# A fused conditional-FFN kernel: the conv's condition term as ScalarE's bias instead of column sums of W, W split by chunk, another unit order in the first iteration

## The chip, the cores and the metric

The kernel runs on one core of a Trainium2 chip. The metric is the device time of one execution in microseconds (us). Each core has TensorE (PE, the matmul engine; PEld is its weight load), VectorE (DVE), ScalarE (ACT), GpSimd (POOL) and SyncE (SP), each with its own queue of instructions, and 16 DMA engines. Engines work in parallel and meet only at semaphores. On-chip memory is SBUF; matmuls write to the banks of PSUM.

## What is computed

Two layers, each adding a feed-forward of a conditional mixing to its input x (128 images, 64 channels, 1024 positions):

```python
x = x + _L0_ffn_ref(_L0_cond_ref(x, cond_128, ...), A, B, bias)   # per-image 64x64 mix + bias, then (.) @ (A @ B.T).T + bias
x = x + _L1_ffn_ref(_L1_cond_ref(x, cond_128, ...), W_up, gate_w, expert_bias, lora_A, lora_B)
# _L1_cond_ref: out = conv1d(x, weight, 9 taps, 4 groups); ctx = c @ c_weight.T
#               out = out + ctx[:, :, None] + bias[None, :, None]
# _L1_ffn_ref:  out @ W_up.T  +  LoRA delta (rank 8) of the one expert that the gate picks (argmax of 4 logits)
```

The condition term ctx + bias is one number for each image and output channel of the conv. It is the same at all 1024 positions.

## The kernel before

The 128 images go in 32 super-steps s of four images; a super-step has two tiles t = 2s and 2s + 1 of 128 rows each. All fp32 products are made of two parts, a rounded high part (fp32r, made by a ScalarE copy) and the low rest (a VectorE subtraction), in three matmuls: high x high, high x low, low x high.

Layer 0 of a super-step: `unit_u` (x times B), `unit_tu` (transposes), `unit_v` (the per-image mix), `unit_o(s, i)` (times A, four banks F0 to F3, into which ScalarE has put the bias). VectorE's `addx` adds the result to x1. SyncE's queue then copies parts of x1 into `Xr` (`rx`, 16 DMAs per super-step), VectorE takes differences (`xd`), ScalarE and VectorE split them (`xs`).

Layer 1, the conv: for each of four groups g, `unit_p(s, g)` makes a product shared by even and odd positions (L778, 3 matmuls, bank F4; in super-step 0 also O1), ScalarE's `pc(s, g)` copies it, doubled, into bank F[g], and `unit_c(s, g)` (L790, 6 matmuls) accumulates on top of it. VectorE transposes the result (`ty`), and `ys` splits it into `yh` and `yl`. Then `step_c(t, c, k)` (L805) multiplies a tile with W (three chunks of 292, 512 and 256 columns, 8 row blocks k each, 3 matmuls per step). The first 36 columns are the gate's and LoRA's; VectorE's `zc` picks the expert, `unit_zt` transposes, ScalarE copies (`zst`), `unit_dl` (L824) adds the LoRA product, and VectorE's `f` adds x1 and writes the output tile.

The condition term is not added to the conv's output in this version. Its effect behind W is: condition value times the sum of W's column block. `wsum` (L840, L841) makes those column sums by 48 matmuls with a matrix of ones in the start-up; they become rows 96 to 98 of `Ls`, the condition values (`cbn`, `cb3`) become columns 96 to 98 of `zs`, so that the LoRA product with 99 rows adds them. For the 36 gate columns `zc` adds `gsB` times `cbn`.

The order on each engine is written out by hand. The loop over `it` runs 32 iterations; iteration `it` has 48 steps n (24 for tile 2·it, 24 for tile 2·it + 1), and between the steps stand the units of later super-steps at fixed n: u(it+2) at 3, tu at 7, v at 9, o(it+2) at 13 to 16, products p(it+1) at 16, 18, 22, 26, convs c(it+1) at 18, 21, 26, 30. Where both stand at one n, the conv comes first. In the start-up, W comes in 8 DMAs, one for each row block with all 1060 columns (`w(k)`: high part by ScalarE, low by VectorE); `wsum`, all of super-step 0's products and convs and o(1) stand ahead of the first step. The lines with the waits that matter here:

```python
def unit_p(s, g):                     # before; s > 0
    if g == 0: pe.wait_ge(v_v, ...)
    elif s > 0: pe.wait_ge(a_pc, 4 * s + g)      # bank F4 is free once ScalarE has copied product g - 1
def unit_c(s, g):
    pe.wait_ge(a_pc, 4 * s + g + 1)
```

## Time and profile before

| | |
|---|---|
| time, median of 3 runs | 1201.2 us (1200.6 to 1202.0) |
| profiled execution | 1200.4 us, span 1198.7 us |
| TensorE busy | 1161.1 us, 97% |
| VectorE busy | 756.0 us, 63% |
| ScalarE busy | 436.8 us, 36% |
| DMA, mean | 127 GB/s; queue 1 takes 46% of the 16 engines |
| granted TensorE clock, mean | 0.988 |

The page gives the busy time of each engine, the span in 40 slices, the DMA queues, the chain of work that ended last, and the costliest groups of instructions by line. TensorE's share of the chain is 94%, most of it in L805. Busy time by stretch tells the start-up from the loop; the chain and the timelines show single instructions and what each waited for. A matmul's duration in a timeline includes its pipeline; what it costs in a row of matmuls is the distance between two starts.

### The profile page before, as it was taken

Reading aid. Unit: us, or ns where it says so; the run is one execution under the profiler, and the core shown is the slowest. Engines: PE = TensorE matmul, PEld = TensorE weight load, DVE = VectorE, ACT = ScalarE, POOL = GpSimd, SP = SyncE. Lnnn points to the kernel's source line nnn. Section 1 sums busy time; section 2 is a strip of 40 time slices with the busy share of each in tenths; the row PEclk is TensorE's granted clock in tenths of the full one; section 3 lists DMA queues with packets and bytes.
Section 4 is the critical chain, followed back from the end, with each engine's and each line's share of the span. In section 5 each row is a group of like instructions: output and inputs, shape, how many; then the busy total and the mean of one; then the engine's idle time right before and its main releaser. Section 6 shows DMA issues by size and latency. Waiting matters only on the chain.

```text
span 1198.7 us, 18813 instructions
## 1 busy us (share of the span) xinstructions
PE 1161.1 (97%) x7460; PEld 1058.4 (88%) x7460; DVE 756.0 (63%) x1511; ACT 436.8 (36%) x669; POOL 8.9 (1%) x22
## 2 busy tenths in 40 slices
PE   6569999999999999999999999999999999999998
PEld 5467999999999999999999999999999999999998
DVE  4847666666766666766566676666667666666652
ACT  5544333334433333433333343333244333334320
POOL 2000000000000000000000000000000000000000
PEclk9789999999999999999999999999999999999999
DMA  9724544544454454445445445544543554544211
GB/s 324 225 63 107 144 113 136 140 117 102 134 147 113 133 142 113 106 135 138 121 133 142 108 107 140 126 130 136 139 101 115 143 114 138 140 124 106 64 52 53
DMA packets 113723, 151.75 MB, mean 127 GB/s; under 512 B 21356, under 2 KB 91500, under 8 KB 109388
## 3 DMA queue, kind: packets, MB, share of 16 engines
q1 hardware_dynamic: 113028, 148.36, 46.4%
q10 hardware_dynamic: 608, 2.20, 0.5%
q8 instruction: 59, 0.97, 0.3%
q14 instruction: 28, 0.23, 0.1%
HBM read 80.87 MB, written 35.68 MB: 97 GB/s over the span
## 4 chain that ended last, share of the span: by engine, by line
PE 94%; DVE 3%; ACT 1%; SPq 1%; DMA 1%; issue 0%; DVEq 0%; ACTq 0%
PE O L805 62%; PE F L790 8%; PE F L758 7%; PE F L778 4%; PE O L824 3%; PE F L730 2%; PE F L729 2%; PE F L728 2%; DVE Wl L588 1%; SPq L222 1%; PE O L816 1%; PE F L745 1%; PE F L746 1%; DMA Xr<-x 0%; DVE wks L609 0%
## 5 line engine op out<-in xcount | busy, mean ns | idle before, releaser
L805 PE MATMUL O<-Wh,yh 128*128 128x292 f32 (+2 forms) x1536 | 510.4, 332 | 0.0
L805 PE MATMUL O<-Wh,yl 128*128 128x292 f32 (+2 forms) x1536 | 498.5, 325 | 0.0
L805 PE MATMUL O<-Wl,yh 128*128 128x292 f32 (+2 forms) x1536 | 498.2, 324 | 0.0
L805 PEld LDWEIGHTS O<-Wh,yh 128*128 128x128 f32 x1536 | 290.0, 189 | 22.9
L805 PEld LDWEIGHTS O<-Wh,yl 128*128 128x128 f32 x1536 | 289.7, 189 | 23.2
L805 PEld LDWEIGHTS O<-Wl,yh 128*128 128x128 f32 x1536 | 290.5, 189 | 17.1
L579 DVE TENSOR_TENSOR osb<-O,x 128x256 f32<-128x256 f32 (+1 forms) x192 | 97.6, 508 | 107.2 <-PE O L824 107.2
L300 ACT ACTIVATE F<-F 128x512 f32<-128x512 f32 x126 | 73.3, 582 | 241.8 <-PE F L778 241.7
L536 DVE STREAM_TRANSPOSE yr<-F 128x512 f32<-128x512 f32 x128 | 91.1, 712 | 58.8 <-PE F L790 58.8
L300 ACT ACTIVATE u<-F 128x256 f32<-128x256 f32 x64 | 24.5, 383 | 267.1 <-PE F L730 223.5
L510 DVE TENSOR_TENSOR x<-F,x 128x512 f32<-128x512 f32 x128 | 87.9, 689 | 36.1 <-PE F L758 36.1
L519 DVE TENSOR_TENSOR Xd<-Xr 128x512 f32<-128x512 f32 x64 | 43.9, 685 | 67.9 <-DMA Xr<-x 67.9
L728 PE MATMUL F<-xTh,Bh 128*128 128x256 f32 x256 | 73.5, 287 | 8.7 <-DVE xTl L478 8.7
L300 ACT ACTIVATE yh<-yr 128x1024 fp32r<-128x1024 f32 x64 | 67.6, 1056 | 32.1 <-DVE yr L536 32.1
L544 DVE TENSOR_TENSOR yl<-yr,yh 128x1024 fp32r<-128x1024 f32 x64 | 77.9, 1218 | 1.8 <-ACT yh L300 1.8
L527 DVE TENSOR_TENSOR Xl<-Xd,Xh 128x1024 fp32r<-128x1024 f32 x64 | 78.0, 1218 | 0.0
L790 PE MATMUL F<-Xh,Th 128*128 128x256 f32 x256 | 75.3, 294 | 1.7 <-ACT F L300 1.7
L478 DVE TENSOR_TENSOR xTl<-xTr,xTh 128x1024 fp32r<-128x1024 f32 x64 | 76.5, 1199 | 0.0
L729 PE MATMUL F<-xTl,Bh 128*128 128x256 f32 x256 | 73.1, 285 | 0.0
L730 PE MATMUL F<-xTh,Bl 128*128 128x256 f32 x256 | 73.0, 285 | 0.0
L790 PE MATMUL F<-Xh,Tl 128*128 128x256 f32 x256 | 71.4, 279 | 0.0
L790 PE MATMUL F<-Xl,Th 128*128 128x256 f32 x256 | 71.3, 278 | 0.0
(139 smaller groups left out, 1520.5 us busy)
## 6 DMA issues: line engine op xcount, KB each, us to landing
x<-in_xP_dram SPq DMA_DIRECT2D x64, 516.0 KB, 4.8
Xr<-x SPq DMA_DIRECT2D x512, 64.5 KB, 2.5
xTr<-in_xT_dram SPq DMA_DIRECT2D x32, 1024.0 KB, 6.5
out_dram<-osb SPq DMA_DIRECT2D x64, 512.0 KB, 2.9
Wr<-in_Wd_dram SPq DMA_DIRECT2D x8, 530.0 KB, 14.1
agb<-agb_scratch SPq DMA_DIRECT2D x31, 128.0 KB, 3.3
agg_scratch<-stage ACTq DMA_DIRECT2D x1, 2048.0 KB, 8.3
agg<-agg_scratch SPq DMA_DIRECT2D x60, 32.0 KB, 2.5
```

Source lines behind the costliest of these rows:

```text
L300: return act.activation(dst, src, ACT.Copy)
L510: dve.tensor_tensor(dst, F[i][:, :].rearrange("p (c a) -> p c a", c=4), dst, ALU.add).then_inc(v_x1, 1)
L527: dve.tensor_tensor(Xl[:, q, 0:2], Xd[:, q, 0:2], Xh[:, q, 0:2].bitcast(fp32), ALU.subtract).then_inc(v_xs, 1)
L536: dve.transpose(yr[:, t % YR].rearrange("p (k r) (g b n) -> p g b k r n", r=2, g=2, b=4)[:, g % 2], F[g][:, :].rearrange("p (b i) -> p b i ...
L544: dve.tensor_tensor(yl[:, t % YR], yr[:, t % YR], yh[:, t % YR].bitcast(fp32), ALU.subtract).then_inc(v_yl, 1)
L579: dve.tensor_tensor(osb[:, lo:hi, :], O[c][:, OFF[c]:CH[c][1]].rearrange("p (c a) -> p c a", c=hi - lo), xs_, ALU.add).then_inc(v_f, 1)
L728: pe.matmul(F[4][:, 0:256], Bh[:, c, :], xTh[:, c, :], start=c == 0, stop=False)
L729: pe.matmul(F[4][:, 0:256], Bh[:, c, :], xTl[:, c, :], start=False, stop=False)
L730: last = pe.matmul(F[4][:, 0:256], Bl[:, c, :], xTh[:, c, :], start=False, stop=c == 7)
L758: last = pe.matmul(F[i][:, :], w[:, q].rearrange("p g b n -> p (g b n)"), m[:, 4 * h:4 * h + 4, :].rearrange("p c a -> p (c a)"), start=Fa ...
L790: last = pe.matmul(dst[:, e], w[:, g, e, :], m[:, g // 2, e, b0:b0 + 4, :], start=False, stop=n_ == 2, skip_group_check=True)
L805: last = pe.matmul(O[c][:, 0:w_], w[:, t % YR, k, :], m[:, k, c0:c0 + w_], start=k == 0 and n_ == 0, stop=k == 7 and n_ == 2)
```

## The change

- The condition term is added at its place: ScalarE's `pc` adds it as a bias column (`cbX`, one value for each partition, group and image) when it copies the shared product. The bias belongs to one image, so the copy of a bank becomes four ACTIVATEs of 128 columns (Identity with a bias column).
- `cbX` is made by four matmuls of 128 columns (`ccX` times condT) behind unit_v(0) and four VectorE additions. `wsum`, `gsB`, `cbn`, `cb3`, three rows of `Ls` and three columns of `zs` go, with their copies.
- W comes in six pieces by chunk and half of the row blocks (`WP`), so that the first chunk can be used before the last has come. `step_c` of tile 0 waits for the piece that it uses.
- Start-up and first iteration get another order on all engines: products 2 and 3, convs 2 and 3 of super-step 0 and o(1) move behind the first steps; the units of super-steps 1 and 2 stand later in iteration 0. `Lr` lies over `osb`; `onesr` and `Xr2` lie elsewhere over `yl`.
- In iterations 1 to 31 the convs stand at 19, 21, 26, 30 (before 18, 21, 26, 30), the products at 16, 18, 22, 26 as before.

```diff
+WP = [(0, 0, 4), (0, 4, 8), (1, 0, 4), (1, 4, 8), (2, 0, 4), (2, 4, 8)]
...
-            return O[1] if s == 0 and g % 2 == 1 else F[4]
+            return O[1 + g % 2] if s == 0 else F[4]
...
-            for k in range(8):
-                sp.dma_start(Wr[:, k, :], Wd[:, k, :]).then_inc(d_w[k], 16)
+            for j, (c, k0, k1) in enumerate(WP):
+                c0, w_ = CH[c]
+                sp.dma_start(Wr[:, k0:k1, c0:c0 + w_], Wd[:, k0:k1, c0:c0 + w_]).then_inc(d_w[j], 16)
...
-                copy(F[g][:, :].rearrange("p (b e i) -> p b e i", b=4, e=2),
-                     pbank(s, g)[:, 0:256].rearrange("p (b i) -> p b i", b=4).unsqueeze(2).broadcast_to([128, 4, 2, 64])).then_inc(a_pc, 1)
+                if s == 0 and g == 0:
+                    act.wait_ge(v_cb, 4)
+                for b in range(4):
+                    last = act.activation(F[g][:, 128 * b:128 * b + 128].rearrange("p (e i) -> p e i", e=2),
+                                          pbank(s, g)[:, 64 * b:64 * b + 64].unsqueeze(1).broadcast_to([128, 2, 64]),
+                                          ACT.Identity, bias=cbX[:, g, 4 * s + b:4 * s + b + 1])
+                last.then_inc(a_pc, 1)
...
+            w(0)
             ut(0)
...
             tuu(0)
-            w(0)
+
+            act.wait_ge(v_wk, 4)
+            w(1)
             vhi(0)
...
             copy(Th[:, :, :, :], Tr[:, :, :, :]).then_inc(a_t, 1)
-            for k in range(1, 4):
-                w(k)
-
-            act.wait_ge(v_wk, 4)
-            w(4)
-            w(5)
             txh(1)
-            w(6)
-            w(7)
-            act.wait_ge(d_l, 16)
-            copy(Ls[0:96, :], Lr[:, :]).then_inc(a_l, 1)
-
-            act.wait_ge(p_cb, 2)
+            w(2)
+            w(3)
+
+            act.wait_ge(p_cb, 1)
...
-                dve.scalar_tensor_tensor(out=zl[:, :], in0=gsB[:, :], scalar=cbn[:, t // 2, t % 2:t % 2 + 1], in1=O[0][:, 0:36],
-                                         op0=ALU.mult, op1=ALU.add).then_inc(v_z, 1)
-                if t > 0:
-                    dve.wait_ge(p_zt, t)
-                dve.tensor_copy(zs[:, 96:99].bitcast(f32r), cb3[:, t, :])
+                dve.tensor_copy(zl[:, :], O[0][:, 0:36]).then_inc(v_z, 1)
...
-                if t == 0 and k == 0:
-                    pe.wait_ge(v_ws, c + 2)
+                if t == 0 and k % 4 == 0:
+                    pe.wait_ge(v_w, 2 * c + k // 4 + 1)
+                if t == 0 and c == 0 and k == 0:
+                    pe.wait_ge(v_cb, 4)
...
-            wsum(0)
-            wsum(1)
-            wsum(2)
-            pe.wait_ge(v_ws, 3)
             unit_p(0, 0)
             unit_p(0, 1)
             unit_c(0, 0)
-            unit_p(0, 2)
             unit_c(0, 1)
-            unit_p(0, 3)
-            unit_c(0, 2)
-            unit_c(0, 3)
-            for i in range(4):
-                unit_o(1, i)
             for it in range(NS):
                 for n in range(48):
                     t = 2 * it + n // 24
                     step_c(t, n % 24 // 8, n % 8)
-                    if n == 3:
+                    if it == 0 and n in (1, 2):
+                        unit_p(0, n + 1)
+                    if it == 0 and n in (3, 4):
+                        unit_c(0, n - 1)
+                    if it == 0 and n in (5, 6, 7, 8):
+                        unit_o(1, n - 5)
+                    if n == (9 if it == 0 else 3):
                         unit_u(it + 2)
...
-                    if n in (18, 21, 26, 30):
-                        unit_c(it + 1, {18: 0, 21: 1, 26: 2, 30: 3}[n])
-                    if n in (16, 18, 22, 26):
-                        unit_p(it + 1, {16: 0, 18: 1, 22: 2, 26: 3}[n])
+                    no = 18 if it == 0 else 13
+                    if no <= n < no + 4:
+                        unit_o(it + 2, n - no)
+                    pp, cc = ((24, 27, 41, 44), (26, 29, 43, 46)) if it == 0 else ((16, 18, 22, 26), (19, 21, 26, 30))
+                    if n in cc:
+                        unit_c(it + 1, cc.index(n))
+                    if n in pp:
+                        unit_p(it + 1, pp.index(n))
```

How the built orders differ at three places. The first is TensorE in an iteration of the loop, from product 0 (first row) on; of three matmuls in a row the first stands. F4 and F0 are PSUM banks, O2 the third chunk's bank. Before:

```order
L778 MATMUL F4<-Xh_85,Th_58 128x256 [waits v_v,v_xs]
...
L805 MATMUL O2<-Wh_49,yh_86 128x256
...
L790 MATMUL F0<-Xh_85,Th_58 128x4x64 [waits a_pc]
...
L778 MATMUL F4<-Xh_85,Th_58 128x256 [waits a_pc]
...
L805 MATMUL O2<-Wh_49,yh_86 128x256
```

After:

```order
L820 MATMUL F4<-Xh_83,Th_58 128x256 [waits v_v,v_xs]
...
L849 MATMUL O2<-Wh_49,yh_84 128x256
...
L820 MATMUL F4<-Xh_83,Th_58 128x256 [waits a_pc]
...
L849 MATMUL O2<-Wh_49,yh_84 128x256
...
L832 MATMUL F0<-Xh_83,Th_58 128x4x64 [waits a_pc]
```

Product 1 now stands ahead of conv 0 with a step between them. Next, ScalarE in an iteration of the loop, the copies of the shared products of one super-step. Before:

```order
L300 ACTIVATE F0<-F4 128x512 [waits v_x1,p_p]
L300 ACTIVATE F1<-F4 128x512 [waits v_x1,p_p]
L300 ACTIVATE F2<-F4 128x512 [waits v_x1,p_p]
L300 ACTIVATE yh_86<-yr_88 128x1024 [waits v_ty]
L300 ACTIVATE F3<-F4 128x512 [waits v_x1,p_p]
```

After:

```order
L369 ACTIVATE F1<-F4,cbX_65 128x128 [waits v_x1,p_p]
L369 ACTIVATE F1<-F4,cbX_65 128x128 x3
L369 ACTIVATE F2<-F4,cbX_65 128x128 [waits v_x1,p_p]
L369 ACTIVATE F2<-F4,cbX_65 128x128 x3
L300 ACTIVATE yh_84<-yr_86 128x1024 [waits v_ty]
L369 ACTIVATE F3<-F4,cbX_65 128x128 [waits v_x1,p_p]
L369 ACTIVATE F3<-F4,cbX_65 128x128 x3
```

Each copy is four instructions; only the last signals TensorE. Last, VectorE in the start-up around the low part of xT(1) (`xTl`). Before:

```order
L510 TENSOR_TENSOR x1_81<-F3,x1_81 128x4x128 [waits p_o]
L588 TENSOR_TENSOR Wl_50<-Wr_51,Wh_49 128x1060 [waits a_w] x4
L478 TENSOR_TENSOR xTl_74<-xTr_75,xTh_73 128x1024 [waits a_txh] x2
L588 TENSOR_TENSOR Wl_50<-Wr_51,Wh_49 128x1060 [waits a_w] x2
L519 TENSOR_TENSOR Xd_84<-Xr_82 128x512 [waits d_rx0]
```

After:

```order
L529 TENSOR_TENSOR x1_79<-F3,x1_79 128x4x128 [waits p_o]
L662 TENSOR_TENSOR Tl_59<-Tr_60,Th_58 128x1536 [waits a_t]
L497 TENSOR_TENSOR xTl_72<-xTr_73,xTh_71 128x1024 [waits a_txh] x2
L607 TENSOR_TENSOR Wl_50<-Wr_51,Wh_49 128x4x512 [waits a_w]
L538 TENSOR_TENSOR Xd_82<-Xr_80 128x512 [waits d_rx0]
```

Ahead of the low part of xT(1) there are now two small pieces of W (292 columns, 4 blocks each), where six of eight stood.

## Rows read from the trace of the kernel before

**Rows 1.** The page, busy time of TensorE: us, share, instructions

```profile
PE 1161.1 (97%) x7460; PEld 1058.4 (88%) x7460; DVE 756.0 (63%) x1511; ACT 436.8 (36%) x669; POOL 8.9 (1%) x22
```

**Rows 2.** Busy time by stretch: length, each engine's busy us, clock, DMA share, GB/s

```profile
0.00:54.00 54.00, 31.76 (x128) 26.15 (x129) 36.18 (x50) 30.24 (x39) 8.89 (x22) 0.87 0.81 267
54.00:100.00 46.00, 34.15 (x177) 29.31 (x177) 24.10 (x42) 19.74 (x30) 0.00 (x0) 0.85 0.41 117
100.00:1190.00 1090.00, 1090.00 (x7125) 998.36 (x7124) 694.22 (x1418) 386.77 (x601) 0.00 (x0) 1.00 0.46 121
44.00:48.00 4.00, 1.47 (x7) 1.47 (x8) 4.00 (x5) 0.00 (x0) 0.00 (x0) 0.50 0.60 101
```

**Rows 3.** The chain in an iteration: start us, length us, what

```profile
519.22 0.11 PE O L816
...
524.23 0.70 PE F L758 x3
524.93 0.35 PE F L778 x3
525.28 0.72 PE O L805 x6
526.00 0.93 PE F L790 x6
...
530.23 1.21 PE O L805 x9
531.44 0.70 PE F L790 x6
...
554.38 0.11 PE O L816
```

**Rows 4.** Timeline of ScalarE in the same iteration: start us, length us, instruction

```profile
525.32 0.58 ACT L300 ACTIVATE F<-F 128x512 f32<-128x512 f32 x1 [2.91 <-PE F L778]
...
529.79 0.58 ACT L300 ACTIVATE F<-F 128x512 f32<-128x512 f32 x1 [1.89 <-PE F L778]
530.28 1.05 ACT L300 ACTIVATE yh<-yr 128x1024 fp32r<-128x1024 f32 x1
```

**Rows 5.** Groups by line: line, engine, operands, count, busy us, mean ns, idle before

```profile
L300 ACT ACTIVATE F<-F 128x512 f32<-128x512 f32 x126 | 73.3, 582 | 241.8 <-PE F L778 241.7
L300 ACT ACTIVATE zst<-O 99x128 fp32r<-99x128 f32 x64 | 17.2, 269 | 91.6 <-PE O L816 91.6
L389 ACT ACTIVATE small<-F,small 128x128 f32<-128x128 f32 x1 | 0.4, 367 | 2.2 <-PE F L845 2.2
```

**Rows 6.** Timeline of TensorE in start-up and first iteration

```profile
20.26 3.60 PE L871 MATMUL O<-small,ccX 128*128 128x32 f32 x16
...
53.47 0.38 PE L840 MATMUL O<-Wh,onesr 128*128 128x292 f32 x1
...
61.31 0.36 PE L778 MATMUL F<-Xh,Th 128*128 128x256 f32 x1
...
75.07 0.30 PE L805 MATMUL O<-Wh,yh 128*128 128x292 f32 x1
...
95.72 0.53 PE L816 MATMUL O<-ident,zs 128*99 128x128 f32 x1 [2.71 <-DVE zs L571]
...
122.09 0.30 PE L805 MATMUL O<-Wh,yh 128*128 128x292 f32 x1
```

**Rows 7.** Timeline of VectorE in the start-up

```profile
44.12 2.35 DVE L478 TENSOR_TENSOR xTl<-xTr,xTh 128x1024 fp32r<-128x1024 f32 x2
...
66.47 1.23 DVE L544 TENSOR_TENSOR yl<-yr,yh 128x1024 fp32r<-128x1024 f32 x1 [1.12 <-ACT yh L300]
```

**Rows 8.** Timeline of ScalarE in the start-up

```profile
38.95 1.90 ACT L300 ACTIVATE xTh<-xTr 128x2048 fp32r<-128x2048 f32 x1
```

**Rows 9.** DMA issues (28 to 29 us; the page): KB, median us to landing

```profile
xTr<-in_xT_dram SPq DMA_DIRECT2D x1, 1024.0 KB, 5.0
...
agg_scratch<-stage ACTq DMA_DIRECT2D x1, 2048.0 KB, 8.3
```

298 lines of the change are left out of this document (164 added, 134 removed).

## The prediction

> **What bounds the kernel now.** First the page's table of busy time: TensorE is busy for 1161.1 of 1198.7 us, 97% [rows 1]. Then busy time by stretch: from 100 to 1190 us TensorE is busy the whole time, and all its idle time (22.2 us to 54 us, 11.9 us from there to 100 us) lies in the start-up [rows 2]. So there are two accounts. In the start-up, less work and fewer waits shorten the time. In the loop, ScalarE and VectorE count only where TensorE waits for them.
>
> Then the chain of waits in one iteration of the loop. One iteration takes 554.38 - 519.22 = 35.16 us [rows 3]. A group of six conv matmuls (L790) takes 0.70 us when nothing holds it, but the first of each iteration takes 0.93 [rows 3]: TensorE comes 0.23 us too early for ScalarE's copy of the shared product. The timeline of ScalarE shows that copy: 525.32 to 525.90, and the chain has the conv at 526.00 [rows 3, 4]. This is the only wait left in an iteration, and it is the place that the change works on.
>
> **Part 1, the copy in the loop.** One ACTIVATE of 128x512 (582 ns [rows 5]) becomes four of 128x128 with a bias column per image. A 128-column copy without a bias column takes 269 ns; a 128-column ACTIVATE with one (the Gelu of the start-up) takes 367 ns [rows 5]. Neighbours overlap by 0.09 us (529.79 + 0.58 against 530.28 [rows 4]). I take the 367 ns, the row that has the bias column: 3 x (0.367 - 0.09) + 0.367 = 1.20 us. The lower bound is the plain copy: 3 x 0.18 + 0.27 = 0.81 us. Rounded, the copy ends 0.62 us later (0.23 at the lower bound).
>
> Who waits for it? By the order of the changed kernel TensorE does product 0, two steps, then product 1, which waits for the copy of product 0 because both use the bank F4; the conv of group 0 comes one step later. Before, conv 0 stood at that same point. So the wait of 0.23 us moves from the conv to product 1 and grows by the full 0.62 us; the later place of conv 0 saves nothing. The other copies have room: from product 1 to conv 1 there are now a step, conv 0 and two steps, 0.36 + 0.70 + 0.72 = 1.78 us. From product 2 to conv 2 there are 1.21 us of first-chunk steps, one step of 0.36 and a product with L of 0.12 [rows 3], 1.69 us in all, against some 1.6 us for drain, copy and weight load. That is about 0.1 us of room: nothing if my 1.20 us is right, a second wait if it is 1.35. The copy with its bias occurs in 30 iterations in this order (the second to the 31st; the last has no next super-step): 30 x 0.62 = **+18.6 us**.
>
> The Trainium skill, page "ScalarE: Activation LUTs", section "What ACT_TABLE_LOAD costs", says that a bias given as a [128,1] pointer adds about 93 ns to an ACTIVATE whatever the function, and that neighbours overlap by about 93 ns. This speaks against the change: by the page's figures, as an estimate, the four take 3 x 0.294 + 0.387 = 1.27 us and the loop loses 30 x 0.69 = 20.7 us. The gap between the two 128-column rows, 98 ns, agrees, but no row before has a copy with a bias column.
>
> **Part 2, what leaves the loop.** The gate's first step on VectorE becomes a plain copy and the cast of three constants goes; 99 rows of the LoRA product become 96, which changes no matmul's columns. TensorE does not wait for VectorE in the loop: 0. Were that cover gone it would be worth some 0.1 us per tile.
>
> **Part 3, the start-up.** The sums of W (L840, L841) fill TensorE from 53.47 to 61.31 us [rows 6]: 7.84 us go. The condition matmuls (3.60 us in a row at 20.26 [rows 6]) become four of 128 columns behind unit v of super-step 0, where TensorE idles; bounded between 0 and that 3.6. I take them as hidden.
>
> The path to the first step of the loop (75.07 us [rows 6]) goes by VectorE's low part of xT(1), at 44.12 us after six of the eight W residuals [rows 7]. Now two residual pieces stand before it, and it waits for data: in the kernel before xT(1) is issued at 28.3 us and lands 5.0 us later [rows 9], at 33.3, behind W and L. The new kernel issues it earlier, behind the same bytes, beside a 2 MB scratch write of 8.3 us [rows 9] that starts some 4 us sooner. I take 35.5 us (bounds 33.3 and 38). The high part of 1.90 us [rows 8] ends at 37.4. From there: 53.47 - 44.12 = 9.35 us to the end of unit v(1) as before (two W pieces stand in both), then from the first product to the low part of y, 66.47 + 1.23 - 61.31 = 6.4 us [rows 6, 7], plus 1.2 for two longer copies and 0.5 for another cast put ahead of y's. The first step starts at 37.4 + 9.35 + 6.4 + 1.7 = 54.9 us, 20.2 us earlier.
>
> Work moves behind that start: four units o(1) of 0.70, two products of 0.35, two convs of 0.70 [rows 3] = 4.9 us. Lead left: 15.3 us.
>
> Waits inside the first iteration: before, it lasted 122.09 - 75.07 = 47.0 us [rows 6], 11.9 us over a steady one, in waits (2.71 us at the gate's transpose, for instance [rows 6]) and half-rate matmuls (granted clock 0.50, the 1.2 GHz level, while TensorE was mostly idle in 44:48 [rows 2]). After, laid out with the same durations: about 3.6 us where products 2, 3 and convs 2, 3 wait for VectorE and the copies, 2.4 at u(2) (xT(2)'s low part stands behind four additions), 1.5 at product 0 of the next super-step, 2.6 at its four convs (0.65 each), 1.9 at the second gate. That is 12.0 us, so nothing is won or lost here; I give it -5 to +5 us, since W's smaller rows (1 to 2 KB instead of 4) and the clock are in it. Start-up: **-15.3 us**, bounds -21 and -10.
>
> **Sum.** -15.3 + 18.6 = +3.3 us. The profiled execution took 1200.4 us (span 1198.7), so 1203.7 there; the median of the runs is 1201.2, 0.8 above it: 1204.5 us.
>
> **Rivals.** All times on the median's footing.
> (a) The bias column costs nothing and the four copies take 0.81 us. For it: the 269 ns row is the same operation on the same memory; the 367 ns may be Gelu's. Loop +6.9, sum -8.4: 1192.8 us. Chance 0.10.
> (b) The other side: the start-up wins as much as the loop loses or more. The place is the first iteration: my 12.0 us of waits come from orders on VectorE that may overlap better, and xT(1) may land at 33.3. The scale tips at a lead of 18.6 us; with 20.5, the sum is -1.9 and the time about 1199 (1196 to 1201.5). For it: 34 us of idle time to win from. Chance 0.25.
> (c) The room of 0.1 us before conv 2 (and conv 3) is gone, 0.1 to 0.2 us more per iteration (+3 to +6), or W's small rows land late and the lead is 11: 1208 to 1212 us. Chance 0.20.
> (d) The clock falls at the longer wait. The 2.71 us wait [rows 6] was followed by half-rate matmuls; the present 0.23 us waits are not, the stretch 100:1190 shows 1.00 [rows 2]. If 0.85 us were enough, each iteration would lose over a microsecond more, 1240 us. Chance 0.03.
> That the change does not do what it says could only be a table load for Identity beside Copy; the built order holds the same two loads as before.
>
> **Numbers.** Forecast 0.42 (1201.5 to 1207.5), (a) 0.10, (b) 0.25, (c) 0.20, (d) 0.03. A measurement of this kernel tells 0.2%, 2.4 us, from no change: faster means under 1198.8, slower over 1203.6. Faster: (a) 0.10, half of (b) 0.13, 0.02 of the forecast = 0.25. Slower: (c), (d) and over half of the forecast = 0.47. Same: 0.28. The range 1196 to 1212 leaves out (a), (d) and tails of (b) and (c), 0.2.
>
> **What would show it.** Right: ACTIVATEs of 128x128 at about 370 ns, each starting 0.28 us after the last; product 1 (L820) waiting some 0.85 us for ScalarE in 30 iterations; a period of 35.8 us; the first step near 55 us and the second iteration near 106.8. Wrong if the period is 35.4 or less (a), the second iteration starts before 103.5 (b), or conv 2 waits too, with a period over 35.9 (c).

## The result: slower, and outside the range

| | before | after |
|---|---|---|
| median of 4 executions | 1201.6 us (1200.6 to 1203.3) | 1225.7 us (1224.8 to 1227.2) |
| span of the profiled execution | 1198.7 us | 1223.4 us |
| TensorE busy | 1161.1 us | 1154.4 us |
| ScalarE busy | 436.8 us | 502.9 us |

The ratio is 1.020 (95% interval 1.018 to 1.022). The forecast was 1204.5 us with a range of 1196 to 1212, so the time lies 13.7 us beyond its upper end. TensorE has less to do, as it should: the 48 matmuls of the column sums are gone. What grew is its waiting: in the loop by about what was forecast, and by some 20 us in the first two iterations, which was not.

The profile after, first the page: the busy time of TensorE, and the group of the new copies (line, engine, operands, count, busy us, mean ns, idle before), which answers to [rows 5]:

```profile
PE 1154.4 (94%) x7404; PEld 1050.1 (86%) x7404; DVE 751.0 (61%) x1440; ACT 502.9 (41%) x1048; POOL 4.9 (0%) x17
...
L369 ACT ACTIVATE F<-F,cbX 128x128 f32<-128x128 f32 x496 | 138.1, 341 | 216.0 <-PE F L820 216.0
```

Busy time by stretch in the kernel after, the view of [rows 2] (length, busy us of each engine with the number of instructions, granted clock, DMA share, GB/s):

```profile
0.00:54.00 54.00, 30.27 (x134) 24.41 (x134) 32.99 (x48) 31.10 (x45) 4.91 (x17) 0.87 0.91 298
54.00:100.00 46.00, 27.71 (x160) 24.11 (x160) 25.44 (x37) 17.68 (x30) 0.00 (x0) 0.87 0.35 81
100.00:150.00 50.00, 40.94 (x236) 36.99 (x237) 28.18 (x52) 19.45 (x43) 0.00 (x0) 0.88 0.42 100
150.00:1190.00 1040.00, 1025.48 (x6689) 937.56 (x6689) 656.68 (x1281) 433.89 (x929) 0.00 (x0) 1.00 0.47 121
```

Read the idle time of TensorE from it. From 54 to 100 us it idles 18.3 us, from 100 to 150 us 9.1 us, where the kernel before had no idle time after 100 us [rows 2], and from 150 us on 14.5 us. The last is the loop; most of the two before it lies in the first and second iterations.

The chain of waits in an iteration of the loop, the view of [rows 3] (start us, length us, what), at the place that the prediction spoke of:

```profile
502.40 0.36 PE F L820 x3
...
503.05 0.86 ACT F L369 x3
...
503.95 0.62 PE F L820 x3
504.57 0.36 PE O L849 x3
504.93 0.70 PE F L832 x6
```

Product 0, then three of the four copies, then product 1 with 0.62 us instead of 0.36. The conv after it takes its plain 0.70 us. That is the wait in its new place, as forecast. TensorE's timeline gives it 0.50 us of idle time, and it comes 29 times from 150 us on, which makes the 14.5 us above; the first matmuls behind a wait also start further apart.

The loop is not where the forecast failed. These are the rows of TensorE's timeline after (start us, length us, instruction, idle time before it and what ended it) for the first step of the loop, the first conv of super-step 1 and the second product of super-step 2:

```profile
56.86 0.40 PE L849 MATMUL O<-Wh,yh 128*128 128x292 f32 x1 [3.15 <-DVE yl L563]
...
101.46 0.58 PE L832 MATMUL F<-Xh,Th 128*128 128x256 f32 x1 [12.07 <-ACT F L369]
...
143.78 0.58 PE L820 MATMUL F<-Xh,Th 128*128 128x256 f32 x1 [4.74 <-ACT F L369]
```

The first step comes 18.2 us earlier than before (75.07 [rows 6]). Then one wait of 12.07 us in the first iteration and one of 4.74 us in the second give all of it back.

**A ruler for all runs.** The transpose of the gate stands at step 12 of every tile; gate t below is that of tile t, so its rows (L860 after) date the same point of the program in every kernel: gate 2 is early in the second iteration, gate 4 early in the third. All times are from each kernel's profiled execution, in us:

| kernel | first step | gate 2 | gate 4 | span | second iteration (gate 2 to 4) | gate 4 to end |
|---|---|---|---|---|---|---|
| before | 75.1 | 132.3 | 167.5 | 1198.7 | 35.2 | 1031.2 |
| after | 56.9 | 132.15 | 174.7 | 1223.4 | 42.5 | 1048.7 |
| e1 | 59.5 | 123.3 | 165.6 | 1214.4 | 42.35 | 1048.8 |
| e2 | 58.1 | 132.4 | 175.1 | 1224.2 | 42.7 | 1049.1 |
| e3 | 57.9 | 133.3 | 174.8 | 1213.9 | 41.5 | 1039.1 |
| e4 | 57.1 | 131.6 | 172.2 | 1205.6 | 40.7 | 1033.4 |
| e5 | 77.7 | 135.6 | 171.8 | 1233.3 | 36.2 | 1061.5 |
| e7 | 55.0 | 131.8 | 172.2 | 1201.4 | 40.35 | 1029.2 |
| e8 | 57.5 | 121.4 | 163.2 | 1192.7 | 41.8 | 1029.5 |
| e9 | 57.9 | 121.5 | 163.55 | 1212.6 | 42.0 | 1049.0 |
| e10 | 58.1 | 120.05 | 163.1 | 1192.3 | 43.0 | 1029.2 |
| e12 | 57.5 | 121.3 | 163.6 | 1212.6 | 42.3 | 1049.0 |
| e13 | 56.0 | 119.8 | 161.3 | 1190.6 | 41.5 | 1029.3 |
| e14 | 76.5 | 135.1 | 170.1 | 1196.5 | 35.0 | 1026.4 |
| e15 | 57.6 | 121.6 | 157.4 | 1207.0 | 35.8 | 1049.6 |
| e16 | 56.2 | 120.15 | 160.1 | 1188.4 | 40.0 | 1028.3 |
| e17 | 75.65 | 126.8 | 161.8 | 1186.3 | 34.9 | 1024.5 |
| e18 | 56.5 | 118.9 | 154.0 | 1182.3 | 35.1 | 1028.3 |
| e19 | 55.9 | 118.9 | 154.0 | 1182.5 | 35.1 | 1028.5 |

The forecast in this ruler, worked out from its own numbers: first step 54.9, gate 2 at 132.3 - 15.3 = 117.0, second iteration 35.16 + 0.62 = 35.8, the rest 1031.2 + 29 x 0.62 = 1049.2, span 1202.0. The miss in span is 21.4 us: 2.0 at the first step, 13.2 between it and gate 2, 6.7 in the second iteration, -0.5 in all the rest.

**Where the 12 us come from.** Three engines' timelines of the kernel after, in order of time; TensorE's wait is the second row above. VectorE ends the low part of x(1, 0) (`xs(1, 0)`):

```profile
86.69 1.22 DVE L546 TENSOR_TENSOR Xl<-Xd,Xh 128x1024 fp32r<-128x1024 f32 x1
```

SyncE, whose queue had stood at this wait (the reload of x(1, 1), `rx(1, 1)`, goes into the same buffer `Xr` and must wait for it), issues its eight transfers, and only behind them xT(3):

```profile
87.98 5.06 SPq L223 DMA_DIRECT2D Xr<-x  x8
93.08 0.59 SPq L182 DMA_DIRECT2D xTr<-in_xT_dram  x1
```

ScalarE stands still for xT(3), and behind its high part come the copies of product 0 (pc(1, 0)):

```profile
98.50 1.91 ACT L300 ACTIVATE xTh<-xTr 128x2048 fp32r<-128x2048 f32 x1 [12.45 <-DMA xTr<-in_xT_dram]
100.32 1.09 ACT L369 ACTIVATE F<-F,cbX 128x128 f32<-128x128 f32 x4
```

The conv follows at 101.46. So the word "ACT" in the row of the conv is true and misleads: the chain behind it is conv, copy, a ScalarE instruction for quite another super-step, a transfer, eight issues on SyncE (0.63 us each), and a residual on VectorE. After the wait the first matmuls run at half rate (the granted clock 0.50 is the 1.2 GHz level); two stretches in the view of [rows 2], behind the first and behind the second of the two waits:

```profile
101.00:105.00 4.00, 3.54 (x15) 3.54 (x16) 2.85 (x4) 0.89 (x4) 0.00 (x0) 0.50 0.27 106
...
143.00:147.00 4.00, 3.22 (x15) 3.22 (x16) 3.55 (x7) 1.84 (x7) 0.00 (x0) 0.50 0.42 65
```

### The profile page after: what moved, and what is told of

The parts are those of the page before. It is cut to its first block, busy times and chain, and to the rows that moved or that the text cites. A ratio compares the mean times of both kernels' runs of the same rounds, so it can differ in the third digit from the quotient of the medians.

```text
span 1223.4 us, 19064 instructions
## 1 busy us (share of the span) xinstructions
PE 1154.4 (94%) x7404; PEld 1050.1 (86%) x7404; DVE 751.0 (61%) x1440; ACT 502.9 (41%) x1048; POOL 4.9 (0%) x17
## 4 chain that ended last, share of the span: by engine, by line
PE 89%; ACT 4%; DVE 2%; DMA 2%; issue 2%; SPq 1%; ACTq 0%
PE O L849 57%; PE F L832 8%; PE F L796 7%; PE F L820 4%; ACT F L369 3%; PE F L766 3%; PE F L767 3%; PE F L768 2%; PE O L867 2%; DMA xTr<-in_xT_dram 2%; SPq L223 1%; PE O L860 1%; PE F L783 1%; PE F L784 1%; ACT xTh L300 0%
## 5 line engine op out<-in xcount | busy, mean ns | idle before, releaser
L369 ACT ACTIVATE F<-F,cbX 128x128 f32<-128x128 f32 x496 | 138.1, 341 | 216.0 <-PE F L820 216.0
L832 PE MATMUL F<-Xh,Th 128*128 128x256 f32 x256 | 73.4, 287 | 14.5 <-ACT F L369 14.4
L766 PE MATMUL F<-xTh,Bh 128*128 128x256 f32 x256 | 74.1, 289 | 13.7 <-DVE xTl L497 13.7
L497 DVE TENSOR_TENSOR xTl<-xTr,xTh 128x1024 fp32r<-128x1024 f32 x64 | 76.5, 1200 | 16.4 <-ACT xTh L300 16.4
L300 ACT ACTIVATE xTh<-xTr 128x2048 fp32r<-128x2048 f32 x32 | 61.1, 1911 | 28.6 <-DMA xTr<-in_xT_dram 28.6
## 6 DMA issues: line engine op xcount, KB each, us to landing
Xr<-x SPq DMA_DIRECT2D x512, 64.5 KB, 2.5
```

The costliest lines, as they stand in the source:

```text
L300: return act.activation(dst, src, ACT.Copy)
L369: last = act.activation(F[g][:, 128 * b:128 * b + 128].rearrange("p (e i) -> p e i", e=2), pbank(s, g)[:, 64 * b:64 * b + 64].unsqueeze(1) ...
L766: pe.matmul(F[4][:, 0:256], Bh[:, c, :], xTh[:, c, :], start=c == 0, stop=False)
L832: last = pe.matmul(dst[:, e], w[:, g, e, :], m[:, g // 2, e, b0:b0 + 4, :], start=False, stop=n_ == 2, skip_group_check=True)
```

## The experiments

The diffs are against the kernel after unless another is named. Medians are of 4 executions (10 in e7). Each group of kernels was measured beside its own 7 to 13 executions of the kernel before, whose medians lay between 1200.7 and 1202.9 us; the ratio is to these. In e3 and e4 a part of the computation is left out, as said there.

| kernel | edit | median us (lowest to highest) | ratio to before, 95% interval |
|---|---|---|---|
| e1 | xT(3), xT(4) issued earlier | 1213.2 (1212.4 to 1216.1) | 1.0096 (1.0079 to 1.0114) |
| e2 | high part of xT(3) behind the copies | 1225.9 (1225.3 to 1227.8) | 1.0206 (1.0191 to 1.0222) |
| e3 | four plain copies | 1215.2 (1214.5 to 1216.0) | 1.0108 (1.0091 to 1.0125) |
| e4 | one plain copy | 1207.6 (1205.6 to 1209.2) | 1.0050 (1.0033 to 1.0068) |
| e5 | before, with four copies with a bias column | 1236.4 (1235.0 to 1236.7) | 1.0283 (1.0267 to 1.0298) |
| e7 | units spread out | 1206.0 (1203.1 to 1210.9) | 1.0039 (1.0025 to 1.0053) |
| e8 | e1 and e7 | 1194.4 (1192.9 to 1196.3) | 0.9942 (0.9926 to 0.9959) |
| e9 | e1, scratch write later | 1214.6 (1214.3 to 1215.3) | 1.0112 (1.0095 to 1.0129) |
| e10 | e8, x(2, 1) behind the additions | 1193.9 (1192.3 to 1195.3) | 0.9932 (0.9915 to 0.9948) |
| e12 | e9, rx(0, 0) ahead of agb(1) | 1214.5 (1213.0 to 1216.2) | 1.0105 (1.0090 to 1.0120) |
| e13 | all of these | 1192.5 (1191.9 to 1193.2) | 0.9921 (0.9907 to 0.9936) |
| e14 | before, units spread out | 1196.4 (1195.4 to 1198.2) | 0.9955 (0.9940 to 0.9970) |
| e15 | second raw buffer | 1206.5 (1205.9 to 1208.8) | 1.0043 (1.0026 to 1.0060) |
| e16 | e13, second raw buffer | 1190.2 (1188.8 to 1190.8) | 0.9907 (0.9892 to 0.9922) |
| e17 | before, units spread out, second raw buffer | 1189.0 (1188.0 to 1189.8) | 0.9898 (0.9884 to 0.9913) |
| e19 | units spread out, second raw buffer | 1185.3 (1184.2 to 1186.1) | 0.9853 (0.9838 to 0.9867) |
| e18 | e19 and the two start-up edits | 1185.3 (1184.0 to 1185.7) | 0.9854 (0.9838 to 0.9871) |

### The first iteration: whose order is it?

**e1**, on SyncE alone:

```diff
             rx(1, 0)
+            load_xT(3)
             rx(1, 1)
             for it in range(NS):
-                load_xT(it + 3)
+                if it > 1:
+                    load_xT(it + 3)
...
                 if it == 0:
+                    load_xT(4)
                     rx(2, 1)
```

> The changed kernel with one thing moved: the transfer of xT(3) is issued on SyncE ahead of the sixteen issues of rx(1, 1), and that of xT(4) ahead of rx(2, 1). In the changed kernel the first conv of the first iteration waits 12.07 us and the second iteration starts at 121.95 us. Theory (order on SyncE's queue: x(1, 1)'s reload waits for the residual of x(1, 0), then issues for 5 us, and only behind it stands xT(3), for which ScalarE stands still ahead of the copy of the product): that wait falls under 3 us, the second iteration starts about 10 to 13 us earlier (109 to 112 us), the extra wait of some 4 us at product 1 in the second iteration goes too, and the time falls by 14 to 20 us, to 1206 to 1212 us. Rival (VectorE or ScalarE hold the conv anyway, since the next thing that is late comes just behind): the wait stays over 7 us and the time falls by less than 8 us, to 1218 or more.

(`rx(1, 1)` is eight issues, not sixteen, as the x8 in SyncE's rows above shows.)

Measured: 1213.2 us, 12.5 less. From gate 0 to gate 2 it takes 123.29 - 81.47 = 41.82 us, where the kernel after has 132.15 - 77.38 = 54.77: 12.95 us are gone, and the conv of the first iteration waits 0.40 us. The theory holds for the first iteration. For the second it does not, and the gain stays a little below what was expected. The rows of e1's TensorE:

```profile
93.88 0.39 PE L835 MATMUL F<-Xh,Th 128*128 128x256 f32 x1 [0.40 <-ACT F L372]
...
135.44 0.58 PE L823 MATMUL F<-Xh,Th 128*128 128x256 f32 x1 [5.26 <-ACT F L372]
```

The second wait is still there, 5.26 us long, although xT(4) now comes early. The timeline of e1's SyncE (start us, us of issuing, instruction) shows why:

```profile
120.68 6.20 SPq L223 DMA_DIRECT2D Xr<-x  x8
```

And the timeline of e1's VectorE:

```profile
128.78 0.69 DVE L541 TENSOR_TENSOR Xd<-Xr 128x512 f32<-128x512 f32 x1 [5.19 <-DMA Xr<-x]
```

The reload of x(2, 1) is issued at 120.68, once x(2, 0) is done with the buffer, and VectorE stands still for it. Behind that stand the additions of x(3, 0) (1.28 us at 133.50), and the copy of product 0 waits for these. So one late thing is gone and the next, with the same root, holds the same unit.

**e2**, on ScalarE alone, with SyncE's order as in the kernel after:

```diff
             for it in range(NS):
...
-                txh(it + 3)
+                if it > 0:
+                    txh(it + 3)
                 pc(it + 1, 0)
                 pc(it + 1, 1)
+                if it == 0:
+                    txh(3)
```

> The changed kernel with one thing moved on ScalarE: in the first iteration the high part of xT(3) stands behind the copies of products 0 and 1 and no longer ahead of them; SyncE's order stays, so xT(3) still lands near 98.5 us. The kernel with xT(3) issued earlier showed the wait of 12.1 us gone (0.4 left) and 12.95 us less from the first gate to the third. Rival (ScalarE's order is a cause by itself): the first conv of the first iteration goes ahead some 10 us earlier and the time falls by 10 us or more, as there. Theory (late data hold whatever stands behind them: VectorE's low part of xT(3) stands ahead of the transposes of the conv, and u(3) in TensorE's order needs it too): the conv's wait goes but turns up again at the next gate or at the low part of y; the time falls by 2 to 8 us, to 1218 to 1224 us.

Measured: 1225.9 us, no gain at all, less than either side expected. That the wait would move and not go was the theory, and that part holds. The conv no longer waits; the gate of tile 1 does, by nearly the same amount:

```profile
110.74 0.45 PE L863 MATMUL O<-ident,zs 128*96 128x128 f32 x1 [11.79 <-DVE zs L591]
```

VectorE, too, has its part of xT(3) ahead of the conv's transposes and of the gate: its row, from e2's timeline, still waits.

```profile
101.53 2.36 DVE L500 TENSOR_TENSOR xTl<-xTr,xTh 128x1024 fp32r<-128x1024 f32 x2 [10.86 <-ACT xTh L300]
```

Here the late transfer held whatever stood behind its first user on each engine. Moving one user in one queue moved the wait and not the end.

### The loop: what the four copies cost

**e3** leaves the condition term out of the computation and copies with four plain copies:

```diff
                 for b in range(4):
-                    last = act.activation(F[g][:, 128 * b:128 * b + 128].rearrange("p (e i) -> p e i", e=2),
-                                          pbank(s, g)[:, 64 * b:64 * b + 64].unsqueeze(1).broadcast_to([128, 2, 64]),
-                                          ACT.Identity, bias=cbX[:, g, 4 * s + b:4 * s + b + 1])
+                    last = copy(F[g][:, 128 * b:128 * b + 128].rearrange("p (e i) -> p e i", e=2),
+                                pbank(s, g)[:, 64 * b:64 * b + 64].unsqueeze(1).broadcast_to([128, 2, 64]))
```

> The changed kernel with the condition term left out of the computation: the four ACTIVATEs with a bias column become four plain copies of 128 columns, everything else as it is. Theory (the price in the loop is made of a part for the bias column and a larger one for the four starts): a plain copy takes about 270 ns, the four 0.81 us instead of 1.11, the wait of product 1 falls by 0.3 us, the period from 35.76 to 35.46 us, and 30 iterations give back 9 us (1216 to 1218 us). Rival (the bias column costs nothing, 341 ns is what 128 columns from PSUM take in this form): period and time stay (35.76 us, 1225).

Measured: 1215.2 us, 10.5 less; from gate 4 to the end 9.6 us less, the period 35.44 us. The group by line of e3's copies:

```profile
L300 ACT ACTIVATE F<-F 128x128 f32<-128x128 f32 x496 | 95.7, 268 | 234.4 <-PE F L819 234.1 <-DVE x L528 0.2
```

Four of them in a row in the timeline of e3's ScalarE:

```profile
535.33 0.77 ACT L300 ACTIVATE F<-F 128x128 f32<-128x128 f32 x4 [3.72 <-PE F L819]
```

A plain copy takes 268 ns and four take 0.77 us, so each adds (0.77 - 0.268) / 3 = 0.167 us. With the bias column it is 341 ns, 1.11 us and 0.256 us. The bias column costs 73 ns in the duration and 89 ns in the distance between two starts.

**e4**, the condition term left out as well, goes back to the single copy, in the new order of units:

```diff
-                for b in range(4):
...
+                last = copy(F[g][:, :].rearrange("p (b e i) -> p b e i", b=4, e=2),
+                            pbank(s, g)[:, 0:256].rearrange("p (b i) -> p b i", b=4).unsqueeze(2).broadcast_to([128, 4, 2, 64]))
```

> The changed kernel with the condition term left out and the product copied by one plain copy of 128x512, as the kernel before did, in the changed order of the units. The four plain copies gave a period of 35.42 us, the four with a bias column 35.76. Theory (product 1 waits until the copy of product 0 ends, and one copy takes 0.58 us where four plain ones take 0.75 to 0.81): period 35.42 - 0.2 = 35.2 us, the same as the 35.16 of the kernel before, and 1225.7 - 29 x 0.55 = about 1209 to 1210 us. Rival (the new order by itself is better or worse than the old one by over 0.1 us per iteration): period under 35.06 or over 35.3.

Measured: 1207.6 us; the period is 544.06 - 508.81 = 35.25 us. The new order by itself gives nothing beside the 35.16 before; if anything it costs the 0.09 us between them. One copy takes the 582 ns of [rows 5]:

```profile
L300 ACT ACTIVATE F<-F 128x512 f32<-128x512 f32 x124 | 72.2, 582 | 245.7 <-PE F L818 243.0 <-DVE yr L553 2.6
```

So of the 0.60 us that an iteration lost, 0.32 lie in the bias columns (35.76 against 35.44), 0.19 in the four starts (35.44 against 35.25), and 0.09 lie between e4 and before, in the order of the units and all else that the change did to the loop. No run parts these.

**e5** puts the four copies with a bias column of zeros into the kernel before and changes nothing else (the tile `zero` is filled in the start-up):

```diff
-                copy(F[g][:, :].rearrange("p (b e i) -> p b e i", b=4, e=2),
-                     pbank(s, g)[:, 0:256].rearrange("p (b i) -> p b i", b=4).unsqueeze(2).broadcast_to([128, 4, 2, 64])).then_inc(a_pc, 1)
...
+                for b in range(4):
+                    last = act.activation(F[g][:, 128 * b:128 * b + 128].rearrange("p (e i) -> p e i", e=2),
+                                          pbank(s, g)[:, 64 * b:64 * b + 64].unsqueeze(1).broadcast_to([128, 2, 64]),
+                                          ACT.Identity, bias=zero[:, 0:1])
+                last.then_inc(a_pc, 1)
```

> The kernel before with one part of the change alone: the copy of the shared product as four ACTIVATEs of 128 columns with a bias column that holds zero; the order of the units, the sums of W and all else stay. Theory (the loop's cost lies in the copy's 0.53 us alone, wherever the unit that waits for it stands): the wait of conv 0 grows from 0.23 to about 0.76 us, the period from 35.16 to 35.69 us, the time by 31 x 0.53 = 16.5 us to about 1218 us; other convs don't wait. Rival (the cost is one of the new order, with product 1 behind two steps): the period stays within 0.2 us of 35.16 and the time under 1208 us.

Measured: 1236.4 us, twice the expected loss. Theory and rival were both wrong. The chain of waits of e5 in one iteration:

```profile
540.45 0.86 ACT F L371 x3
...
541.35 0.98 PE F L797 x6
542.33 0.36 PE F L785 x3
...
542.98 0.86 ACT F L371 x3
...
543.89 0.97 PE F L797 x6
```

Conv 0 waits, and conv 1 waits too: the three steps between product 1 and conv 1 (1.05 us) hide a copy of 0.58 us but not one of 1.11, so the chain goes by the copies twice. The period is 554.33 - 518.12 = 36.21 us, 1.05 more than before. The changed order, with conv 0 a step later and so behind product 1's wait, pays once and not twice. With the four copies the changed loop takes 36.21 - 35.76 = 0.45 us less in each iteration than the old one.

**e7** spreads the units of the second and later iterations out:

```diff
-                    pp, cc = ((24, 27, 41, 44), (26, 29, 43, 46)) if it == 0 else ((16, 18, 22, 26), (19, 21, 26, 30))
+                    pp, cc = ((24, 27, 41, 44), (26, 29, 43, 46)) if it == 0 else ((16, 20, 24, 28), (20, 24, 28, 32))
```

> The changed kernel with the units of the iterations from the second on spread out: products at steps 16, 20, 24, 28 and convs at 20, 24, 28, 32, so that four steps lie between a product and the next; the first iteration as it is. Theory (the loop's whole cost is TensorE's wait for the copies, and the 1.11 us of copying can be covered by steps): product 1 no longer waits, the period falls from 35.76 to about 34.93 us, under the 35.16 of the kernel before, and the time by 29 x 0.83 = 24 us to about 1201 us. Rival (what is moved behind collides with VectorE's additions and the low part of y, which the next tile needs): the wait turns up at conv 3 or at the next tile's first step and the time falls by less than 12 us.

Measured: 1206.0 us, 19.7 less where 24 were expected. Its ten executions spread from 1203.1 to 1210.9 us, and the profiled one was the fastest. Two gates that stand an iteration apart:

```profile
507.33 0.27 PE L860 MATMUL O<-ident,zs 128*96 128x128 f32 x1
...
542.41 0.27 PE L860 MATMUL O<-ident,zs 128*96 128x128 f32 x1
```

The period is 35.08 us, under the 35.16 before, and not the expected 34.93. From 150 to 1190 us the waits list no line. Seven units that stand one to three steps later hide nearly all of the price of the copies; 0.15 us per iteration over the 34.93 stay that no row names.

**e8** is e1 and e7 together.

> The two single edits together: xT(3) and xT(4) issued ahead of the reloads they stood behind, and the units of the second iteration onward spread out (products at 16, 20, 24, 28, convs at 20, 24, 28, 32). Alone they gave -12.5 us (1213.2) and -19.7 us (1206.0). If they lie in different places of the program, as the theory has it (first iteration; loop), they add up: 1225.7 - 32.2 = 1193.5 us, 8 us below the kernel before. Rival (each takes away part of the same wait in the second iteration): 1198 or more.

Measured: 1194.4 us against an expected 1193.5. The two lie in different places and add up, though with e7's spread the agreement within 1 us is partly luck. Its second iteration keeps 41.8 us.

### The start-up: what sets the first step

**e9** is e1 with the scratch write behind the high part of xT(1) on ScalarE:

```diff
             vhi(0)
-            act.dma_start(aggD.rearrange("n i o -> n (i o)"), stage[:, :]).then_inc(d_gw, 16)
             act.wait_ge(v_t, 1)
             copy(Th[:, :, :, :], Tr[:, :, :, :]).then_inc(a_t, 1)
             txh(1)
+            act.dma_start(aggD.rearrange("n i o -> n (i o)"), stage[:, :]).then_inc(d_gw, 16)
```

> The kernel with xT(3) and xT(4) issued earlier (1213.2 us) and one more thing: ScalarE issues the 2 MB write of the scratch copy of the aggregates behind the high part of xT(1), no longer ahead of it. In the changed kernel the write went out at 27.05 us, took 12.8 us, and xT(1) landed at 38.0 (36.3 to 40.3 in the runs so far), 13.6 us after its issue, where 5.0 were seen before. Theory (the write takes bandwidth from xT(1), so the predicted landing of 35.5 was missed): xT(1) lands at 33 to 35 us, the first step comes 2 to 5 us earlier, the time falls to 1209 to 1211 us. Rival (xT(1) is late because W's and L's bytes stand ahead of it in the same queue): the landing stays at 37 to 38 us and the time within 1 us of 1213, or above it, since the write itself is now late for the loads that wait for it.

Measured: 1214.6 us, no gain. xT(1) did come early, at 33.5 us (ScalarE's row), and then VectorE waited for the reload of x(0, 0), and the first step came at 57.86. First the row of e9's ScalarE:

```profile
33.49 1.91 ACT L303 ACTIVATE xTh<-xTr 128x2048 fp32r<-128x2048 f32 x1 [3.78 <-DMA xTr<-in_xT_dram]
```

Then VectorE's first difference of x(0, 0) in e9:

```profile
44.03 0.69 DVE L541 TENSOR_TENSOR Xd<-Xr 128x512 f32<-128x512 f32 x1 [4.03 <-DMA Xr<-x]
```

And the first step of the loop on e9's TensorE:

```profile
57.86 0.61 PE L852 MATMUL O<-Wh,yh 128*128 128x292 f32 x1 [3.16 <-DVE yl L566]
```

This fits the theory that the write holds xT(1) up. In the five kernels with this edit the high part of xT(1) starts at 32.9 to 36.2 us, in ten without it at 33.7 to 40.3, nine of them over 36, from one profiled execution each. It is the consequence for the time that fails.

**e12** is e9 with rx(0, 0) issued ahead of the load of agb(1):

```diff
-            load_agb(1)
             rx(0, 0)
+            load_agb(1)
             rx(0, 1)
```

> The kernel with xT(3), xT(4) earlier and the scratch write behind the high part of xT(1) (1214.6 us), and one more thing: SyncE issues the eight transfers of the reload rx(0, 0) ahead of the load of agb(1), which waits for a write of ScalarE's to land. In that kernel xT(1) landed at 33.5 us, 4.6 us earlier than in the changed kernel, and still the first step came at 57.9 us (56.9 in the changed kernel), VectorE having waited 4.0 us for the reload of x(0, 0) at 44.0 us. Theory (the reload, 16 issues of 0.83 us behind the wait for agb, is what the first step comes from once xT(1) is early): the reload starts some 2 us earlier, x(0, 0) lands near 42 us, the first step comes at 55.5 to 56.5 us, the time falls by 1.5 to 2.5 us to about 1212.5 us. Rival (something else, such as agb(1) or the product's own waits, sets it): no change, 1214 to 1215.

Measured: 1214.5 us, no change. The reload began to be issued at 31.15 us, and x(0, 0) was taken up at 44.19 all the same, as in e9. The first step needs xT(1) and x(0, 0) both, and over all the kernels with the change it lay between 55.0 and 59.5 us, with no order by these edits (55.0 is e7, which has neither). The spread of one execution to the next is thus as large as the 2.0 us by which the first step missed. It doesn't explain the miss away: all fifteen lie above the forecast 54.9, by 2.3 us in the mean.

### The second iteration and the buffer

**e10** is e8 with the work on x(2, 1) taken back behind the additions on VectorE and behind the first two copies on ScalarE:

```diff
                 txh(it + 3)
                 pc(it + 1, 0)
                 pc(it + 1, 1)
+                if it == 1:
+                    xs(2, 1)
...
                     addx(it + 2, 0)
                     addx(it + 2, 1)
+                    if it == 1:
+                        xd(2, 1)
                     f(t, 0)
+                    if it == 1:
+                        xs(2, 1)
```

The calls of xd(2, 1) and xs(2, 1) that stood further ahead are gone; the first hunk is ScalarE's order, the second VectorE's.

> The two edits together (xT(3), xT(4) earlier; units spread out: 1194.4 us) and one more in the second iteration alone: VectorE and ScalarE take the differences and rounding of x(2, 1) behind the additions of x(3, 0) and x(3, 1) and the copies of products 0 and 1, no longer ahead of them. In the kernel with both edits the span from the third gate to the fifth is 147.50 + 15.73 - 121.39 = 41.8 us against 35.1 in a steady iteration, a loss of 6.8 us. There VectorE stands still for 5.2 us until the reload of x(2, 1) has landed, and the additions, for which the copy of product 0 waits, stand behind it. Theory (that standing still, and not the reload itself, holds TensorE): the wait of some 4 to 5 us and the half-rate matmuls behind it go, third gate to fifth takes 35 to 37 us, and the time falls by 4 to 7 us to 1187.5 to 1190.5 us. Rival (the reload is needed by products 2 and 3 of the same iteration anyway, so it only moves): the wait turns up at product 2 and the time falls by less than 2 us.

Measured: 1193.9 us, 0.5 less than e8, inside the spread: the rival. The wait went to the third product, the first that needs x(2, 1), and to a gate:

```profile
133.38 0.58 PE L824 MATMUL F<-Xh,Th 128*128 128x256 f32 x1 [2.27 <-DVE Xl L549]
...
145.74 0.31 PE L864 MATMUL O<-ident,zs 128*96 128x128 f32 x1 [2.31 <-DVE zs L591]
```

**e13** is everything so far together.

> All edits at once: xT(3), xT(4) earlier, units spread out, x(2, 1) behind the additions in the second iteration, the scratch write behind the high part of xT(1), rx(0, 0) ahead of agb(1). Theory (each removes a wait of its own): 1194.4 less 5 (second iteration) less 1 to 2 (start-up) = 1187 to 1188.5 us. Rival (the last two gain nothing together): within 1 us of the kernel without them.

Measured: 1192.5 us, 1.4 under e10. Expected were 1187 to 1188.5, and the rival said within 1 us. The two start-up edits are worth 1.4 us at most, and by e18 below nothing.

What e1, e2 and e10 have in common: each moves one thing in one queue, and the reload keeps waiting for the buffer. **e15** takes away what makes it wait, with all orders as in the kernel after:

```diff
         Xr = sb("Xr", [128, 8, 129])
+        XrB = sb("XrB", [128, 8, 129])
...
-            return Xr2 if s == 0 and q == 1 else Xr
+            if q == 1:
+                return Xr2 if s == 0 else XrB
+            return Xr
...
                 if s > 0:
-                    sp.wait_ge(v_xs, 2 * s + q)
+                    sp.wait_ge(v_xs, 2 * s + q - 1)
```

> The changed kernel with a second buffer for the raw reload of the odd tiles: rx(s, 1) goes into a buffer of its own and waits for xs(s - 1, 1) and no longer for xs(s, 0). No order is changed. Theory (both losses behind the first step have one root, that rx(1, 1) and rx(2, 1) can't be issued before the residual of the even tile, and xT(3), xT(4) stand behind them on SyncE): the 12.07 us wait of the first iteration falls under 1 us, and the second iteration, which kept its loss of 6.6 us when only xT was moved ahead, loses less than 3; the time falls by 16 to 20 us to 1206 to 1210 us. Rival (the second iteration's loss has another cause, such as the additions of x(3, 0)): the time is that of the kernel with xT(3), xT(4) moved, 1213 us.

Measured: 1206.5 us, 19.2 less, as expected. Two rows of the timeline of e15's SyncE:

```profile
73.33 5.25 SPq L226 DMA_DIRECT2D XrB<-x  x8
78.62 0.59 SPq L185 DMA_DIRECT2D xTr<-in_xT_dram  x1
```

Gates 2 and 4 in the timeline of e15's TensorE:

```profile
121.56 0.27 PE L863 MATMUL O<-ident,zs 128*96 128x128 f32 x1
...
157.36 0.27 PE L863 MATMUL O<-ident,zs 128*96 128x128 f32 x1
```

The reload of x(1, 1) goes out at 73.33 (before the residual of x(1, 0) is even begun) and xT(3) at 78.62 and not 93.08. Gate 2 comes 10.6 us earlier, and the second iteration takes 35.80 us, the steady period. Both losses have one root: a single buffer, 4 KB per partition too little. Up to gate 2 e15 takes 63.9 us from its first step, the forecast 62.1 and the kernel after 75.3, so 11.4 of the 13.2 us are gone.

**e16** is e13 with the second buffer.

> The kernel with all edits so far (1192.5 us) and the second buffer for the raw reload of the odd tiles. Theory: its second iteration takes 41.5 us from the third gate to the fifth (119.84 to 161.34) against 35.1 in a steady one, since products 2 and 3 wait for the reload of x(2, 1); with the second buffer this goes, and the time falls by 4 to 6 us to 1186.5 to 1188.5 us. Rival (other waits come just behind): under 2 us.

Measured: 1190.2 us, 2.3 less and not 4 to 6. Its third product still waits 2.3 us for VectorE's residual of x(2, 1), and VectorE has waited 6.0 us there for ScalarE, which has x(2, 1) behind two copies: the edit of e10, no gain when it was made, costs something once its reason is gone.

### What the change is worth when nothing else is in the way

**e14** and **e17** are the kernel before with the units spread out, and with the second buffer besides. **e19** is the kernel after with the same two edits, and **e18** is e19 with the start-up edits of e9 and e12.

> The kernel before with the units spread out as in the fastest of these kernels (products at steps 16, 20, 24, 28, convs at 20, 24, 28, 32 of every iteration), and nothing of the change. Its one wait in an iteration is the 0.23 us of conv 0. Theory (spread out, the loop's period is TensorE's own work whichever copy is used): the period falls from 35.16 to 34.9 to 35.1 us and the time by 2 to 7 us, to 1195 to 1199 us. Then the loop is the same with and without the change, and what the change can be worth is its start-up alone. Rival (the spread order has a cost of its own that the changed kernel hides): 1200 us or more.

Measured: 1196.4 us, period 539.30 - 504.31 = 34.99 us, as expected.

> The kernel before with the units spread out (1196.4 us) and the same second buffer, nothing of the change. Its first and second iteration show no wait of that kind (third gate to fifth 34.99 us, a steady one). Theory (the single buffer costs only where the start-up is early, as in the changed kernel): no gain, 1195 to 1197.5 us. Rival (the first iteration of the kernel before loses by it too): 1193 us or less.

Measured: 1189.0 us, 7.4 less than e14: the expectation was wrong. The kernel before lost to the single buffer too. In its first iteration VectorE stood still, with the gate of tile 0 behind it (row of the kernel before):

```profile
92.63 0.69 DVE L519 TENSOR_TENSOR Xd<-Xr 128x512 f32<-128x512 f32 x1 [7.21 <-DMA Xr<-x]
```

In e17 the same instruction comes at 86.41 after 0.55 us. The 2.71 us of the gate in [rows 6] was the visible end of that wait. From the first step to gate 0 e17 takes 16.3 us and e14 20.8; from there to gate 2 34.9 and 37.9.

> The changed kernel with the second raw buffer and the units spread out (products at 16, 20, 24, 28, convs at 20, 24, 28, 32 from the second iteration on), no other edit. The kernel before with the same two edits took 1189.0 us, so this is the change alone on equal footing. With the second buffer alone the changed kernel took 1206.5 us, its second iteration steady at 35.80 us. Theory (the period goes to 35.08 us, 30 x 0.70 = 21 us less, and the first iteration keeps its 41.8 us between the first and third gates): 1185.5 to 1187 us, 2 to 3 us below the kernel before with the same edits. Rival (a wait in the second iteration as in the kernel with all edits, 4.9 us): 1190 us or more.

Measured: 1185.3 us, level with e18, and 1.5% below the kernel before. Gate 4 is at 154.01 us in e19 and at 161.76 in e17, a lead of 7.75 us; from there to the end e19 takes 1028.5 us and e17 1024.5. The change wins 7.75 us in the start-up and pays 4.0 in the loop, which is the difference of their periods, 29 x 0.14 = 4.1 us. These are gates 4 and 6 of e17, a period of 34.93 us, and then of e19, 35.07:

```profile
161.76 0.27 PE L819 MATMUL O<-ident,zs 128*99 128x128 f32 x1
...
196.69 0.27 PE L819 MATMUL O<-ident,zs 128*99 128x128 f32 x1
```

```profile
154.01 0.27 PE L863 MATMUL O<-ident,zs 128*96 128x128 f32 x1
...
189.08 0.27 PE L863 MATMUL O<-ident,zs 128*96 128x128 f32 x1
```

What the 0.14 us are is open; neither kernel shows a wait there. The first step of e19 is 19.7 us earlier, and 11.8 of these are spent again by gate 2: from its first step to there TensorE is busy 8.5 us longer than in e17 (4.9 us are the work moved behind the first step) and idle 3.3 us longer.

The ratios to the kernel before are 0.9853 and 0.9898, with intervals that don't overlap, so the change alone is worth about 0.45% on this footing, some 4 to 5 us (3.7 by the medians).

> As before, with the two start-up edits too (scratch write behind the high part of xT(1), rx(0, 0) ahead of agb(1)), and without the edit that put x(2, 1) behind the additions. Theory (the start-up edits are worth the 1 to 1.5 us by which they beat the kernel without them, 1193.9 to 1192.5): 1184 to 1186 us, the fastest of all. Rival (they are worth nothing once xT(3) comes early): the same as without them within 0.5 us.

Measured: 1185.3 us, the same as e19: the rival. The start-up edits are worth nothing.

## The prediction, point by point

**The price of the copies in the loop: right, its size partly by luck.** Forecast 1.20 us for the four and +0.62 us per iteration; measured 1.11 and +0.60 (1048.7 - 1031.2 = 17.5 us over 29 iterations). The copies grew by 0.53 us and not by 0.62; the 0.09 us between e4 and before, which the sum doesn't have, made up for it. It named the instruction that waits (product 1) and said that conv 0 would not and that convs 2 and 3 have enough room. The lower bound was near as well (0.81 from the plain copy; e3 measured 0.77). The estimate from the figures of the Trainium skill, page "ScalarE: Activation LUTs", section "What ACT_TABLE_LOAD costs", was 1.27 us: measured 1.11. Its 93 ns for a bias pointer agrees with the 89 ns between starts; the duration estimated from its figures is too long here (387 ns for 128 columns, measured 341).

**"The later place of conv 0 saves nothing": right with one copy, wrong with four.** Compared with one copy it saves nothing (e4). Compared with four copies in the old order (e5) the changed loop takes 0.45 us less per iteration. The prediction did not ask what the old order would have done with the new copy, though the order and the copy came in one change.

**Part 2 held, and rivals (a) and (d) did not come.** VectorE's smaller gate gave TensorE nothing: e4's period is no shorter than that of the kernel before. The bias column is not free (e3). The waits of the loop don't lower the clock: 150:1190 shows 1.00 in the kernel after, with 29 of them. Behind the waits of 4.74 and 12.07 us it stood at 0.50.

**The first step: 56.9 and not 54.9**, a miss of 2.0 us, and for an incomplete reason. The sum put the start at the landing of xT(1), forecast 35.5 and measured 38.0. e9 shows that an earlier xT(1) is caught by the reload of x(0, 0), for which the sum has no term.

**Waits inside the first iteration: the step that failed.** "That is 12.0 us, so nothing is won or lost here", with bounds of 5 us either way. Measured: 13.2 us more up to gate 2. The waits on VectorE that it listed came nearly to size: 2.35 us at u(2) for 2.4, 1.25 at product 0 for 1.5, 1.78 at the second gate for 1.9. The convs' were smaller (0.4 to 0.5 us each in e19 for 0.65). What it left out, and so put at nothing, is SyncE's queue. The reload `rx(1, 1)` waits for the residual of x(1, 0), because both use `Xr`, and with it waits all that SyncE has behind it, xT(3) above all. In the kernel before the same buffer made its reload late as well, but that cost less: taking it away gave 7.4 us there (e17 beside e14) and 19.2 here (e15). So the 11.9 us of excess that the prediction read from [rows 6] and put against its own 12.0 already held some of this loss. e1 and e15 show the failed step, the one by taking xT(3) out of the queue, the other by taking away the wait.

**The second iteration: not in the sum at all.** It was taken as steady. It lost 6.7 us more than forecast, to the same buffer (e15: 35.80 us).

**The sum of it.** The wait in the loop and its arithmetic were right; what was missing was one wait on a queue that does no arithmetic. With the second buffer the kernel takes 1206.5 us, 2 us over the forecast and within its range. That is no proof of the sum, for the forecast was made from the kernel before, whose own loss to the buffer is in it. Rival (b) looked at the very place, the first iteration, and expected it only to be better than the sum; no rival let it be worse by more than the bounds.

## What to carry to other kernels

When a change makes an early stage start sooner, lay out every queue anew from there, the DMA queue first: for each transfer the buffer that it fills and the last reader of that buffer, and what stands behind it. A lead won ahead of a single buffer can be lost at that buffer: here most of the 18.2 us were. If a wait survives two reorderings and turns up elsewhere each time, look for what is late for all of them: here 4 KB of memory per partition gave 19.2 us, where three reorderings (e1, e2, e10) gave 12.5, nothing and 0.5.

A longer copy costs little when the work that needs it stands far enough behind it. Measure a copy's price in the order in which it will run; the same four ACTIVATEs cost 1.05, 0.60 and about 0.1 us per iteration in three orders.

## What was not expected of the hardware

- Four ACTIVATEs in a row with a bias column are 0.256 us apart at 128 columns, plain ones 0.167 us, though their durations are 341 and 268 ns.
- Small issues on SyncE's queue weigh: 16 transfers of 64.5 KB took 13.3 us to issue in the start-up of the kernel after (0.83 us each in the mean, with the DMA engines busy for 0.83 of that stretch) and 0.63 us each ahead of xT(3). The six pieces of W took 11.5 us to issue, the eight row blocks of the kernel before, the same bytes, 5.8 us.
- In the profiled executions of ten kernels that issue the same start-up, the high part of one transfer (xT(1)) started anywhere between 33.7 and 40.3 us, and the first step of the loop between 55.0 and 59.5 us, not in step with it (e8: 33.7 and 57.5; e7: 36.3 and 55.0).
